# Gate logits of a fused attention and expert kernel: the gate weights held still in four column tiles

## What is computed

```python
x = x + attention(layernorm(x), ctx, ctx, mask)          # 16 heads, d_k = 32
xf = layernorm(x).reshape(8192, 512)
scores = softmax(xf @ w_gate)                             # w_gate: 512 x 8
weights, idx = top_k(scores, 2)
# each token is gathered into the lists of its two experts (capacity 2048)
h = silu(exp_x @ fc_a) * (exp_x @ fc_g)                   # per expert, 512 -> 768
out = sum over the two experts of weight * (h @ c_proj)   # 768 -> 512
x = x + out
```

## Time and profile before

| what | us |
|---|---|
| median of three runs | 3083.16 |
| lowest and highest | 3080.51, 3084.50 |
| the profiled execution, its own time | 3081.46 |
| its span, first to last instruction | 3079.70 |

### The profile page before, as it was taken

One profiled execution on the slowest core, in us unless ns is written; L12 is line 12 of the kernel. 1 busy time (PEld: TensorE's weight loads), 2 busy tenths in 40 slices (PEclk: granted clock), 3 DMA queues, 4 the chain that ended last, 5 costly groups with the idle time before them and its releaser, 6 DMA issues.

```text
span 3079.7 us, 55845 instructions
## 1 busy us (share of the span) xinstructions
PE 2998.1 (97%) x18336; PEld 2537.2 (82%) x18336; DVE 1448.5 (47%) x4906; ACT 1523.5 (49%) x3910; POOL 1259.1 (41%) x1913
## 2 busy tenths in 40 slices
PE   6999999999999999995999999999999999999998
PEld 6888888888888888874888888888888888888886
DVE  5777777777777777763223222131232221312321
ACT  4777778777778777772223232232232322322321
POOL 4666666666666667652121222221222222121211
PEclk9999999999999999997999999999999999999999
DMA  5444444444444445433232323232323333333212
GB/s 166 119 130 128 130 123 129 120 125 133 130 122 125 126 122 133 123 82 132 48 82 48 76 56 76 50 81 52 79 52 72 59 72 53 79 54 77 43 27 28
DMA packets 216664, 281.83 MB, mean 92 GB/s; under 512 B 38336, under 2 KB 161216, under 8 KB 214848
## 3 DMA queue, kind: packets, MB, share of 16 engines
q1 hardware_dynamic: 153312, 144.89, 17.6%
q0 software_dynamic: 32768, 67.26, 12.8%
q10 hardware_dynamic: 30304, 66.07, 6.7%
HBM read 109.53 MB, written 67.90 MB: 58 GB/s over the span
## 4 chain that ended last, share of the span: by engine, by line
PE 52%; DMA 1%; issue 0%; POOL 0%; ACT 0%; SPq 0%; DVE 0%; POOLq 0%
PE a_ps L1211 17%; PE g_ps L1211 17%; PE y_ps L1226 17%; PE turn_ps L1187 2%; DMA pj_raw<-in_c_proj 1%; DMA out<-y,recs 0%; DMA xg<-xn_rows,gather_ids 0%; POOL xg L1045 0%; DMA lists<-table 0%; POOL out L1073 0%; ACT L1119 0%; SPq L994 0%; DVE hidden L1167 0%; ACT y L1133 0%; ACT pj_hi L1094 0%
## 5 line engine op out<-in xcount | busy, mean ns | idle before, releaser
L1073 POOL DMA_INDIRECT out<-y,recs x128 | 204.9, 1601 | 1243.3 <-ACT y L1133 926.1
L371 POOL TENSOR_SCALAR probs<-probs,row_inv 128x256 f32<-128x256 f32 x1024 | 489.3, 489 | 418.1 <-DVE row_inv L584 413.7
L1167 DVE TENSOR_TENSOR hidden<-act_part,g_ps 128x512 f32<-128x512 f32 x192 | 132.2, 688 | 1001.5 <-ACT act_part L1119 1001.5
L575 DVE CUSTOM_DVE_ANT_0 probs<-scores_ps,mask_add,row_any 128x256 f32<-128x256 f32 x1024 | 454.8, 481 | 266.7 <-PE scores_ps L791 262.9
L475 ACT ACTIVATE probs<-probs,low 128x256 f32<-128x256 f32 x1024 | 513.9, 504 | 106.6 <-DVE low L575 93.2
L1119 ACT ACTIVATE act_part<-a_ps 128x512 f32<-128x512 f32 x192 | 114.8, 598 | 675.0 <-PE g_ps L1211 675.0
L460 ACT COPY probs_t<-probs_t_ps 128x512 f32<-128x512 f32 x512 | 299.6, 585 | 186.1 <-PE probs_t_ps L803 137.6
L803 PE MATMUL probs_t_ps<-ident,probs 128*128 128x128 f32 x2048 | 310.1, 273 | 7.0 <-POOL probs L371 6.9
L1211 PE MATMUL a_ps<-xe_hi,fc_hi 128*128 128x512 f32 x768 | 312.3, 407 | 4.3 <-DVE hidden L1167 2.9
L1211 PE MATMUL a_ps<-xe_hi,fc_lo 128*128 128x512 f32 x768 | 301.6, 393 | 0.0
L1211 PE MATMUL a_ps<-xe_lo,fc_hi 128*128 128x512 f32 x768 | 300.7, 392 | 0.0
(11 more groups left out here) (167 smaller groups left out, 6612.4 us busy)
## 6 DMA issues: line engine op xcount, KB each, us to landing
k_stack<-qk_hi SPq DMA_DIRECT2D x512, 64.0 KB, 2.0
q_stack<-qk_hi SPq DMA_DIRECT2D x512, 64.0 KB, 2.9
fc_raw<-in_c_fc SPq DMA_DIRECT2D x24, 1024.0 KB, 5.7
k_stack<-qk_lo SPq DMA_DIRECT2D x256, 64.0 KB, 2.0
q_stack<-qk_lo SPq DMA_DIRECT2D x256, 64.0 KB, 2.9
out<-x_xn ACTq DMA_DIRECT2D x32, 512.0 KB, 3.3
xn_rows<-x_xn ACTq DMA_DIRECT2D x32, 512.0 KB, 3.7
cin<-in_ctx_t ACTq DMA_DIRECT2D x31, 512.0 KB, 4.1
```

Source lines behind the costliest of these rows:

```text
L371: last = nc.gpsimd.tensor_scalar(probs[:, r, t, :], probs[:, r, t, :], row_inv[:, r, t:t + 1], 1.0, ALU.mult, ALU.mult)
L575: last = nc.vector.tensor_tensor_reduce(out=probs[:, s % 4, t, :], in0=scores_ps[s % 2][:, t, :], in1=mask_add[:, t, :], scale=row_any[:, ...
L1073: nc.gpsimd.indirect_dma_start(out=out[:, :], out_offset=bass.IndirectOffsetOnAxis(ap=recs[:, i * CT + t, 0:1].bitcast(U32), axis=0), in_= ...
L1167: nc.vector.tensor_tensor(hidden[:, m % 2, :], act_part[:, m % 2, :], g_ps[m % 2][:, :], ALU.mult).then_inc(gated, 1)
```

## The change

The roles of the gate's operands are exchanged. `wg` gets 32 columns per chunk, of which 8 are the gate's and 24 zeros (GpSimd clears it, and the load on SyncE waits for that). In slot 12 four matmuls hold one chunk of `wg` each, 128 x 32, in column tiles 0, 32, 64 and 96, and stream all 256 tokens; their results lie in four groups of 32 partitions of `bank_b`, not yet added up. ScalarE copies them to `gate_parts` (128 x 256). In slot 13 two matmuls hold `gate_parts`, 128 tokens each, and stream `sum_parts`, 8 columns with a one in rows e, 32 + e, 64 + e and 96 + e: this adds the four parts and gives the logits in the place and layout that they had.

Since both halves of `x2t` must be there in slot 12, the transposes move to slots 10 and 11, both into `bank_a`, the second after ScalarE's copy of the first; in slot 11 they stand ahead of the L818 group.

```diff
-        wg = sb("wg", [P, DC, EXPERTS])
+        wg = sb("wg", [P, DC, DK])
+        sum_parts = sb("sum_parts", [P, EXPERTS])
+        gate_parts = sb("gate_parts", [P, SEQ])
...
-                        sp.dma_start(wg[:, :, :], w_gate).then_inc(setup_loaded, 16)
+                        sp.wait_ge(wg_cleared, 1)
+                        sp.dma_start(wg[:, :, 0:EXPERTS], w_gate).then_inc(setup_loaded, 16)
...
+                nc.gpsimd.memset(wg[:, :, :], 0.0).then_inc(wg_cleared, 1)
...
+                nc.gpsimd.memset(sum_parts[:, :], 0.0).then_inc(sum_parts_ready, 1)
+                for c in range(DC):
+                    pool.wait_ge(sum_parts_ready, c + 1)
+                    nc.gpsimd.affine_select(out=sum_parts[:, :], in_=sum_parts[:, :], compare_op=ALU.not_equal,
+                                            fill=1.0, base=-c * DK, pattern=[[-1, EXPERTS]],
+                                            channel_multiplier=1).then_inc(sum_parts_ready, 1)
...  ScalarE
-                        if s in (10, 12) and tail:
-                            t = (s - 10) // 2
+                        if s in (10, 11) and tail:
+                            t = s - 10
                             act.wait_ge(x2_stored, n * 16)
                             act.wait_ge(x2t_full, n * TILES - TILES + t + 1)
-                            nc.scalar.copy(x2t[:, :, t * P:(t + 1) * P], (bank_a, bank_b)[t][:, :].rearrange(
+                            nc.scalar.copy(x2t[:, :, t * P:(t + 1) * P], bank_a[:, :].rearrange(
                                 "p (c i) -> p c i", c=DC)).then_inc(x2t_ready, 1)
+                        if s == 12 and tail:
+                            act.wait_ge(gate_full, n)
+                            need(act, logits_full, n - 1)
+                            nc.scalar.copy(gate_parts[:, :], bank_b[:, 0:SEQ]).then_inc(gate_copied, 1)
...  TensorE
+                        if s in (10, 11) and tail:
+                            t = s - 10
+                            pe.wait_ge(xn2_ready, n)
+                            if t:
+                                pe.wait_ge(x2t_ready, (n - 1) * TILES + 1)
+                            elif proj:
+                                pe.wait_ge(k_ready, (n + 1) * DC + DC)
+                            else:
+                                pe.wait_ge(v_ready, BATCH * TILES)
+                            transposed(bank_a, xn2, t, x2t_full)
...
-                        if s in (10, 12) and tail:
-                            ...
-                            transposed((bank_a, bank_b)[t], xn2, t, x2t_full)
+                        if s == 12 and tail:
+                            if proj:
+                                pe.wait_ge(q_ready, (n + 1) * DC + 2)
+                            else:
+                                pe.wait_ge(x2_ready, (n - 1) * TILES + 1)
+                            pe.wait_ge(x2t_ready, n * TILES)
+                            for c in range(DC):
+                                last = nc.tensor.matmul(bank_b[c * DK:(c + 1) * DK, 0:SEQ], wg[:, c, :],
+                                                        x2t[:, c, :], start=True, stop=True)
+                            last.then_inc(gate_full, 1)
                         if s == 13 and tail:
-                            pe.wait_ge(x2t_ready, n * TILES)
+                            pe.wait_ge(gate_copied, n)
                             for t in range(TILES):
-                                for c in range(DC):
-                                    last = nc.tensor.matmul(bank_b[:, t * EXPERTS:(t + 1) * EXPERTS],
-                                                            x2t[:, c, t * P:(t + 1) * P], wg[:, c, :],
-                                                            start=(c == 0), stop=(c == DC - 1))
+                                last = nc.tensor.matmul(bank_b[:, t * EXPERTS:(t + 1) * EXPERTS],
+                                                        gate_parts[:, t * P:(t + 1) * P], sum_parts[:, :],
+                                                        start=True, stop=True)
                             last.then_inc(logits_full, 1)
...
                                 if tail:
-                                    pe.wait_ge(x2t_ready, (n - 1) * TILES + 1)
+                                    pe.wait_ge(x2t_ready, n * TILES)
```

More of the change, by code:

```diff
@@ L220, in attention_block @@
         x2t_ready = sem("x2t_ready")
+        wg_cleared = sem("wg_cleared")
+        sum_parts_ready = sem("sum_parts_ready")
+        gate_full = sem("gate_full")
+        gate_copied = sem("gate_copied")
         logits_full = sem("logits_full")
@@ L833, in step @@
                             transposed((bank_a, bank_b)[t], xn, t, xt_full)
-                        if s in (10, 12) and tail:
-                            t = (s - 10) // 2
-                            pe.wait_ge(xn2_ready, n)
-                            if not proj:
-                                pe.wait_ge(v_ready, BATCH * TILES)
-                            elif t:
-                                pe.wait_ge(q_ready, (n + 1) * DC + 2)
-                            else:
-                                pe.wait_ge(k_ready, (n + 1) * DC + DC)
-                            if not heads:
-                                pe.wait_ge(x2_ready, (n - 1) * TILES + 1)
-                            transposed((bank_a, bank_b)[t], xn2, t, x2t_full)
-                        if s == 13 and tail:
+                        if s == 12 and tail:
                             if is_step(n, 1):
```

3 lines of the change are left out of this document (added).

## The result

The changed kernel takes 3067.66 us in the median of five runs (3064.52 to 3068.99), against 3083.16 of the kernel before (3079.38 to 3086.46, also five). The ratio is 0.9949, with a 95% interval from 0.9938 to 0.9961: 15.5 us less, and the whole interval lies beyond the 0.2% that a measurement can tell from no change. The forecast was 3067.4. The profiled run of the changed kernel took 3064.52 us with a span of 3062.7; it is the one whose rows stand here, beside the 3081.46 and 3079.7 of the run of before. Its lines of code are 20 higher than those of before in TensorE's part: L823 is the transposing of probabilities (L803), L766 that of `xn2` (L746), L848 the attention group (L818), L775 and L789 the projections (L755, L769). L875 are the four gate tiles and L883 the sum with ones.

A forecast was written before the change was run, and what follows sets the result against it. TensorE, busy 1234.95 of 1235.00 us in the full steps, was taken as the bound: 30 x 0.59 = 17.7, less 1.6 (slot 14) and 0.3 (start), gains 15.8 us, giving 3067.4 us; forecast's own range 3064 to 3071, 8-in-10 range 3061.5 to 3077.

The forecast's parts named there:

- What goes: Slot 13 on TensorE: twelve of sixteen gate records go, at the weight loads' pace of 0.111 each, 1.33 us per step.
- the even share: Slot 13's other pricing: an even share of the gate's 1.70 us for sixteen records, giving 1.28 instead of 1.33.
- What comes: TensorE's added work: tile block 0.56, entering it 0.09, moved transposes 0.09, together 0.74 us per step.
- the 0.62: Upper bound of TensorE's net gain per step, forecast at 0.59; also used in the rival of a 19.5 us gain, chance 0.09.
- the rival in series: Gate tiles run one behind the other: block 1.87 us instead of 0.56, each step loses 0.72, 3105 us; chance 0.05.
- Slot 14: TensorE comes 0.59 earlier to its wait for VectorE's low part of q: short room in ten steps, 1.6 us of waits.
- VectorE's 0.44 of delay: VectorE's slot 12 mask comes 0.44 later but inside its idle time before the x load (mean 0.93), so its time doesn't change.
- The room of 0.9: Slot 12: ScalarE's second x2t copy ends about 618.80, the tile block comes at 619.74, so TensorE should not wait.
- The q stacks: Slot 0: last copy lands at 628.4 in the median, 629.7 at most, read at 629.74; no wait expected, a rare one possible.
- 17.7 - 1.6: The 30 full steps: 30 x 0.59 = 17.7 us gained on TensorE, less 1.6 of waits in slot 14.
- step 31: Step without projections, standing in the chain of one head, where TensorE's gain may vanish: 0, bounds 1 us either way.
- the last gate: Step 32, one chain: some 2.6 us less from slow loads, against wait 0.9, tile block 1.0, copy and handing over 0.7: 0, bounds 0.5.

The follow-up runs named there:

- a quarter of the gate: Kernel before with only one of the gate's four feature chunks (two matmuls instead of eight), part of the computation left out: 3059.04 us; with late moments 3047.8.
- joined blocks: Changed kernel, slot 11's attention group behind the q projection, gate tiles directly behind: 3064.08 us with late moments, 3066.01 with early; late moments and x2t copy first, 3057.34.
- late moments: Changed kernel with VectorE's moments of the loaded x in slot 14 instead of 12 and GpSimd's root in slot 15 instead of 13: 3065.96 us.
- the one with a single tile: Changed kernel with the four gate matmuls accumulated in one column tile, ScalarE copying 32 partitions and the sum reading 32 rows: 3114.73 us.
- the changed kernel's second profile: The changed kernel run once more, nothing altered, on the same chip as two other kernels: 3066.67 us, ratio 0.9951.

## Why the prediction was right

**What goes.** 1.33 us forecast; slot 13 lost 1.323, and 1.34 with a quarter of the gate. The pace of the weight loads was the right price, and the even share (1.28) would have been too low.

**What comes.** 0.74 forecast, with 0.76 as the upper bound; slots 11 and 12 together gained 0.412 + 0.353 = 0.765. The sum was right to 0.03. Not all of its parts were: the block itself is 0.57 for 0.56, its entry costs 0.18 and not 0.09, and the move of the transposes nothing instead of 0.09. The prediction had compared the transposes' old 0.35 with their new 0.44, without asking what takes the 0.35 when they are gone. These make 0.75, and the second projection matmul behind the block, which comes 0.34 behind the first (613.57 - 613.23) instead of 0.31 or 0.32 elsewhere, makes about the rest. The net of a step's edit is 1.323 - 0.765 = 0.558, where 0.59 was forecast with 0.52 and 0.62 as bounds; for the 0.62 the prediction gives no working.

On the way the Trainium skill's sentence that a change of the tiling mode drains TensorE (TensorEngine Tiling (Array Packing), Tiling Modes) fits what the runs show: the joined blocks, which spare one entry and one exit, take 0.43 us for the tiles where the separate block takes 0.75. No run shows the drain itself. The Trainium skill's sentence on weight loads (TensorE: Matmul & The Clock Gate, Part 3), that they overlap running matmuls only where the row group differs, which the prediction took to bring four tiles that share all rows nearer to the rival in series, is not borne out: the tiles take 0.57 us against the 1.84 of a true series.

**Slot 14.** 1.6 us forecast in ten steps; in ten steps TensorE's weight load does follow VectorE's end, and it is late by 1.6 us in all. By the slot's lengths, which hold some 0.3 of other things, the same is 2.07, and 1.0 and 1.3 in two other runs. Place, mechanism and size were right; that this one run gives the very number is luck, as runs differ by more. The assumption under it, that VectorE's 0.44 of delay would vanish in its wait for x, shows in 15.5 us of such waiting instead of 26.9: 29 times 0.44 would be 12.8, and 11.4 went. That the load of x is the cause was shown by moving the moments behind L603.

**ScalarE and the q stacks.** No TensorE wait in the view names a ScalarE copy in the full steps. The room of 0.9 was 0.76, by the 0.14 of handing over that the prediction had left out. The q stacks cost nothing in the changed kernel. With the late moments alone they cost one wait, and with the quarter of the gate besides they became the next limit.

**The full steps.** 17.7 - 1.6 = 16.1 forecast, 15.7 measured. By slots: 1.323 - 0.765 - 0.070 - 0.021 = 0.467 a step are explained, and 0.056 come from slots 0 to 10, where nothing was changed. It is 1.7 us in 30 steps and comes with the new gate: slots 0 to 10 take 26.90 to 26.93 us in eight of the nine other runs with it, the one with a single tile included, and 26.97 to 26.98 in those with the old gate in which nothing waits there. Its cause stays open. The prediction had no such term, so that the full steps came within 0.4 us of the forecast is partly luck: what is explained gives 14.0 us of the 16.1.

**The ends.** For step 31 the forecast had 0, with bounds of 1 either way, and for the last gate 0 with 0.5: together they came to a loss of 0.87, within the bounds. 0.43 of it is the last gate's chain, from the first transposes to the copy of the logits: 1402.71 - 1396.67 = 6.04 before, 1386.97 - 1380.50 = 6.47 after. The timeline of this place, answering to the earlier trace rows:

```profile
1380.50 1.12 PE L766 MATMUL bank_a<-ident,x_xn 128*128 128x128 f32 x4 [4.76 <-DVE x_xn L563]
...
1382.44 1.09 PE L766 MATMUL bank_a<-ident,x_xn 128*128 128x128 f32 x4 [0.82 <-ACT x_xn L485]
...
1384.35 1.08 PE L875 MATMUL bank_b<-x_xn,wg 128*32 128x256 f32 x8 [0.82 <-ACT x_xn L485]
...
1386.97 0.17 DVE L669 COPY logits<-bank_b 128x16 f32<-128x16 f32 x1 [6.52 <-PE bank_b L883]
```

From the gate's start to the logits it is shorter by 1.0 (2.62 for 3.62), much as worked out (2.6 less, 1.0 and 0.7 more). The second transposes, however, start 1.94 behind the first (1382.44 - 1380.50) instead of 0.63 before (1397.30 - 1396.67), since they wait for the copy that empties their bank: 1.31 is lost, where 0.9 had been put in. From their start to the gate's start it is 0.12 more. The other 0.44 lies ahead of the first transposes. There the mean granted clock was lower, by the busy time by stretch from the start of step 31 to the last gate, first before and then after:

```profile
1345.85:1402.31 56.46, 44.07 (x290) 33.30 (x288) 30.13 (x131) 31.25 (x94) 28.72 (x48) 0.86 0.21 63
```

```profile
1329.24:1386.57 57.33, 42.95 (x282) 30.74 (x280) 30.36 (x133) 32.36 (x98) 28.79 (x49) 0.81 0.18 54
```

That the clock is the cause is argued and not shown. For it speaks that the changed kernel's second profile has 57.28 at 0.81, the one with late moments 57.91 at 0.81, the one with the transposes behind the attention group 57.97 at 0.78, the one with another copy on ScalarE 56.50 at 0.83, and the joined blocks 58.35 and 58.18 at 0.81. The quarter of the gate has 54.29 at 0.82, with less work in the chain. The transposes moved alone, with the whole old gate, have 58.44 at 0.80, so it isn't the lighter gate alone that goes with a lower clock. What lowers it wasn't tried.

## What to carry to other kernels

Where one engine is busy for all of a stretch, price an edit by that engine's starts, and ask of everything that is moved or put in what then stands beside it: a short block's cost is partly its neighbours', and blocks of column tiles belong directly behind others of the same tiling, since the way in and out costs as much as one to two rounds. Then read the room at each wait behind the edit in every step and not in one: here the next limit came at some 0.6 us a step (a load in front of a small operation) and the one after it between 0.9 and 1.3 (a transfer), and the second could be seen only when the first was gone.

## What the runs showed of the hardware

- Four gate tiles of 128 x 32 stationary and 256 float32 columns take 0.57 us alone between full-size matmuls and 0.43 directly behind another block of the same tiling; in one tile, accumulated, 1.84. The entry costs 0.18 behind transposes (0.53 to the block where a projection follows after 0.35).
- A stationary of 32 rows and 128 columns between full-size matmuls has a price of its own (the kernel with one tile): four records of 8 columns start 0.53 behind the transposes and take 0.54, against 0.44 and 0.37 with 128 rows, though it has a quarter of the rows.
- Where TensorE waits for a 512-column copy of ScalarE out of PSUM, it starts 0.14 to 0.15 us after the end that the trace gives the copy.
